# The second norms' variances and inverse deviations, four tiles at a time, on GpSimd instead of VectorE

## The reference

```python
h = patches(x) @ W                                   # 64 images, 36 tokens each, 192 channels
h = h + attention(layernorm(h))                      # 12 heads of 16, causal over the 36 tokens
h = h + experts(layernorm(h))                        # 8 experts, 192 -> 768 -> 192, the best 2 per token
# layernorm: (x - mean) / sqrt(var + 1e-5), over the 192 channels, no weights
```

## Time and profile before

| | |
|---|---|
| time, median of 3 runs | 413.14 us (410.65 to 414.38) |
| profiled execution | 408.58 us, its span 406.8 us |
| TensorE busy | 367.6 us, 90% |
| VectorE busy | 255.3 us, 63% |
| ScalarE busy | 218.6 us, 54% |
| GpSimd busy | 167.7 us, 41% |
| mean granted TensorE clock | 0.964 |

### The profile page before, as it was taken

The page is one execution under the profiler, slowest core; times in us unless marked ns, Lnnn a source line. Parts: engine busy times, 40 slices in busy tenths (PEclk is TensorE's granted clock), DMA queues, the critical chain, the costliest instruction groups (busy, mean ns, idle before and its releaser), DMA issues.

```text
span 406.8 us, 14803 instructions
## 1 busy us (share of the span) xinstructions
PE 367.6 (90%) x5699; PEld 327.6 (81%) x5699; DVE 255.3 (63%) x687; ACT 218.6 (54%) x442; POOL 167.7 (41%) x203
## 2 busy tenths in 40 slices
PE   3989999989999999899897999999999999999910
PEld 3989989979889999885453689999999999999800
DVE  3696477787877867788686254555545554455426
ACT  5667687768777687662344244444444444444400
POOL 8116333345375532422100555555555555553310
PEclk9999999999999899999896999999999999999975
DMA  8974024432334223443060213222223222122058
GB/s 264 314 247 156 15 56 133 135 95 75 118 111 119 84 59 111 117 132 86 27 171 12 60 31 90 61 81 61 80 60 90 81 60 81 60 55 47 31 205 337
DMA packets 29705, 42.81 MB, mean 105 GB/s; under 512 B 12416, under 2 KB 19440, under 8 KB 29640
## 3 DMA queue, kind: packets, MB, share of 16 engines
q1 hardware_dynamic: 25512, 33.37, 27.1%
q0 software_dynamic: 4128, 8.50, 7.4%
HBM read 30.23 MB, written 9.67 MB: 98 GB/s over the span
## 4 chain that ended last, share of the span: by engine, by line
PE 75%; DVE 14%; DMA 3%; ACT 3%; issue 2%; POOL 2%; SPq 0%; POOLq 0%; DVEq 0%; ACTq 0%
PE PSA L1415 19%; PE PSA L1430 15%; PE PSA L1169 6%; PE PSA L1111 6%; PE PSA L1143 5%; PE PSA L1195 4%; PE PSA L1264 4%; PE PSA L1219 3%; PE PSA L1155 2%; PE PSA L1434 2%; PE PSA L1180 2%; PE PSA L1382 2%; DMA W2l<-yrows 2%; DVE H L1098 1%; PE PSA L1164 1%
## 5 line engine op out<-in xcount | busy, mean ns | idle before, releaser
L1415 PE MATMUL PSA<-YT,W1h 128*128 128x128 f16 x774 | 78.0, 219 | 1.5 <-DVE YT L1060 1.5
L1415 PE MATMUL PSA<-YT,W1l 128*128 128x128 f16 (+1 forms) x516 | 75.3, 220 | 0.0
L1430 PE MATMUL PSA<-W2h,PTR 128*128 x516 | 70.9, 246 | 0.3 <-DVE PTR L744 0.3
L543 POOL DMA_INDIRECT yrows<-KBR x43 | 43.1, 1001 | 63.4 <-DVE KBR L1075 63.4
L1415 PEld LDWEIGHTS PSA<-YT,W1h 128*128 x774 | 63.7, 98 | 5.6 <-DVE YT L1060 1.8
L1430 PE MATMUL PSA<-W2l,PTR 128*128 x258 | 63.5, 246 | 0.0
L730 ACT ACTIVATE PTR<-PSA 128x768 f32<-128x768 f32 x43 | 34.9, 812 | 51.1 <-PE PSA L1415 51.1
L538 POOL DMA_INDIRECT REG<-xrows,KBR x43 | 42.4, 987 | 43.6 <-DVE KBR L1050 27.4
L735 ACT ACTIVATE PTR<-PTR 128x768 f16<-128x768 f32 x43 | 36.3, 845 | 44.3 <-PE PSA L1434 44.2
L744 DVE SCALAR_TENSOR_TENSOR PTR<-PTR 128x768 f16<-128x768 f32 x43 | 41.2, 958 | 24.8 <-ACT PTR L735 24.8
L1075 DVE TENSOR_SCALAR KBR<-PSA,KBR 128x192 f32<-128x192 f32 x43 | 17.9, 417 | 52.9 <-PE PSA L1434 52.9
(11 more groups left out here) (179 smaller groups left out, 798.5 us busy)
## 6 DMA issues: line engine op xcount, KB each, us to landing
WSTG<-w SPq DMA_DIRECT2D x16, 384.0 KB, 3.9
WSTG<-w SPq DMA_DIRECT2D x16, 336.0 KB, 3.3
REG<-xt SPq DMA_DIRECT2D x12, 324.0 KB, 4.6
W1l<-xt SPq DMA_DIRECT2D x10, 324.0 KB, 6.8
VB<-VP SPq DMA_DIRECT2D x99, 19.1 KB
H<-hrows SPq DMA_DIRECT2D x6, 288.0 KB, 2.8
xrows<-REG SPq DMA_DIRECT2D x2, 800.2 KB
hrows<-H SPq DMA_DIRECT2D x1, 1296.0 KB
```

Of the source, the lines that this page charges most:

```text
L543: gp.indirect_dma_start(out=yrows, out_offset=bass.IndirectOffsetOnAxis(ap=TARGET[:, s:s + 1], axis=0), in_=YO[s % 2], in_offset=None).the ...
L1415: ins = nc.tensor.matmul(bank(2 * u + f // (FC // 2), 128, FC // 2 * ST_)[:, w:w + ST_], weights[a, c], YT[0:rows, at:at + ST_], start=k = ...
L1430: nc.tensor.matmul(bank(4 + u, ST_, C), GP[a][:, at:at + ST_], weights[b], start=(f, a, b) == (0, 0, 0), stop=False)
```

## The change

For groups 2 to 5, GpSimd computes what VectorE's `variances` and `refine` did. GpSimd's version has twelve operations instead of ten: each of the two fused operations of VectorE (square with a factor, add with multiply) is two. It runs them in the group step behind `norm1_row` and ahead of `norm2_row`. In between it waits for ScalarE's logarithm and exponential, which now wait for GpSimd's seventh operation. Groups 6 and 7 and the first norm stay on VectorE; the counts of VectorE's semaphores are shifted accordingly (`on_vector`).

```diff
+        ON_GPSIMD = range(2, group(PAIRED))
+        PSTEPS = 12
...
+            def group_variances(n):
+                a, b = NORMS[n]
+                base = PSTEPS * (n - ON_GPSIMD.start)
+                gp.wait_ge(st2_done, b - NT)
+                s = ST[:, a * 6:b * 6].rearrange("p (t c) -> p t c", c=6)
+                mean, dm, var = MEAN[:, a:b], DM[:, a:b], VAR[:, a:b]
+                nc.gpsimd.tensor_tensor(mean, s[:, :, 1], s[:, :, 4], ALU.add).then_inc(group_done, 1)
+                nc.gpsimd.tensor_tensor(dm, s[:, :, 1], s[:, :, 4], ALU.subtract).then_inc(group_done, 1)
+                nc.gpsimd.tensor_tensor(var, s[:, :, 2], s[:, :, 5], ALU.add).then_inc(group_done, 1)
+                gp.wait_ge(group_done, base + 2)
+                nc.gpsimd.tensor_tensor(dm, dm, dm, ALU.mult).then_inc(group_done, 1)
+                gp.wait_ge(group_done, base + 4)
+                nc.gpsimd.tensor_scalar(dm, dm, 0.25 * C, None, ALU.mult).then_inc(group_done, 1)
+                nc.gpsimd.tensor_scalar(mean, mean, 0.5, None, ALU.mult).then_inc(group_done, 1)
+                gp.wait_ge(group_done, base + 5)
+                nc.gpsimd.tensor_tensor(var, var, dm, ALU.add).then_inc(group_done, 1)
+                gp.wait_ge(group_done, base + 7)
+                nc.gpsimd.tensor_scalar(HV[:, a:b], var, -0.5 / (C * S_X ** 2), -0.5 * EPS / S_X ** 2, ALU.mult, ALU.add).then_inc(group_done, 1)
+
+            def group_refine(n):
...
+                gp.wait_ge(ln_done, 2 * n + 2)
+                gp.wait_ge(group_done, base + 8)
+                nc.gpsimd.tensor_tensor(t1, rs, HV[:, a:b], ALU.mult).then_inc(group_done, 1)
+                gp.wait_ge(group_done, base + 9)
+                nc.gpsimd.tensor_tensor(t1, t1, rs, ALU.mult).then_inc(group_done, 1)
+                gp.wait_ge(group_done, base + 10)
+                nc.gpsimd.tensor_scalar(t1, t1, 1.5, None, ALU.add).then_inc(group_done, 1)
+                gp.wait_ge(group_done, base + 11)
+                nc.gpsimd.tensor_tensor(rs, t1, rs, ALU.mult).then_inc(group_done, 1)
+
             def norm2_row(t):
-                need(gp, rs_done, group(t) + 1)
+                if group(t) in ON_GPSIMD:
+                    gp.wait_ge(group_done, PSTEPS * (group(t) - ON_GPSIMD.start + 1))
+                else:
+                    need(gp, rs_done, on_vector(group(t)) + 1)
...
                 if has(i + 6):
                     norm1_row(i + 6)
+                if group_end(i - 2) and group(i - 2) in ON_GPSIMD:
+                    group_variances(group(i - 2))
+                    group_refine(group(i - 2))
                 for t in norm2_at(i):
                     norm2_row(t)
...
             def inverse_deviation(n):
                 a, b = NORMS[n]
-                act.wait_ge(mv_done, 9 * n + 7)
+                if n in ON_GPSIMD:
+                    act.wait_ge(group_done, PSTEPS * (n - ON_GPSIMD.start) + 7)
+                else:
+                    act.wait_ge(mv_done, 9 * on_vector(n) + 7)
...
                     stats2(i - 2)
-                    if group_end(i - 2):
+                    if group_end(i - 2) and group(i - 2) not in ON_GPSIMD:
                         variances(group(i - 2))
...
-                if group_end(i - 2):
+                if group_end(i - 2) and group(i - 2) not in ON_GPSIMD:
                     refine(group(i - 2))
```

More of the change, by code:

```diff
@@ L215, in build @@
         st_done, st2_done, mv_done, ln_done, rs_done = [sem(n) for n in ("st_done", "st2_done", "mv_done", "ln_done", "rs_done")]
+        group_done = sem("group_done")
         n1_row, n1_hi, n1_lo, n1_mm, n1_done = [sem(f"norm1_{n}") for n in ("row", "hi", "lo", "mm", "done")]
@@ L345, in build, with on_vector @@
         NORMS += [(NT + t, NT + min(t + GROUP, NT)) for t in range(0, NT, GROUP)]
+        ON_GPSIMD = range(2, group(PAIRED))
+        PSTEPS = 12
+        def on_vector(n):
+            return n - len(ON_GPSIMD) if n >= ON_GPSIMD.stop else n
         def up_biases(p):
@@ new lines, in group_refine @@
+            def group_refine(n):
+                a, b = NORMS[n]
+                base = PSTEPS * (n - ON_GPSIMD.start)
+                rs, t1 = RS[:, a:b], DM[:, a:b]
+                gp.wait_ge(ln_done, 2 * n + 2)
[7 more added lines that the diff above has]
+                nc.gpsimd.tensor_tensor(rs, t1, rs, ALU.mult).then_inc(group_done, 1)
@@ L774, in variances @@
                 nc.vector.tensor_tensor(var, s[:, :, 2], s[:, :, 5], ALU.add).then_inc(mv_done, 1)
-                dve.wait_ge(mv_done, 9 * n + 3)
+                dve.wait_ge(mv_done, 9 * on_vector(n) + 3)
                 nc.vector.tensor_scalar(mean, mean, 0.5, None, ALU.mult).then_inc(mv_done, 1)
                 nc.vector.scalar_tensor_tensor(dm, dm, 0.25 * C, dm, ALU.mult, ALU.mult).then_inc(mv_done, 1)
-                dve.wait_ge(mv_done, 9 * n + 5)
+                dve.wait_ge(mv_done, 9 * on_vector(n) + 5)
                 nc.vector.tensor_tensor(var, var, dm, ALU.add).then_inc(mv_done, 1)
-                dve.wait_ge(mv_done, 9 * n + 6)
+                dve.wait_ge(mv_done, 9 * on_vector(n) + 6)
                 nc.vector.tensor_scalar(HV[:, a:b], var, -0.5 / (C * S_X ** 2), -0.5 * EPS / S_X ** 2, ALU.mult, ALU.add).then_inc(mv_done, 1)
@@ L787, in refine @@
                 nc.vector.tensor_tensor(t1, rs, HV[:, a:b], ALU.mult).then_inc(mv_done, 1)
-                dve.wait_ge(mv_done, 9 * n + 8)
+                dve.wait_ge(mv_done, 9 * on_vector(n) + 8)
                 nc.vector.tensor_tensor(t1, t1, rs, ALU.mult).then_inc(mv_done, 1)
-                dve.wait_ge(mv_done, 9 * n + 9)
+                dve.wait_ge(mv_done, 9 * on_vector(n) + 9)
                 nc.vector.scalar_tensor_tensor(rs, t1, 1.5, rs, ALU.add, ALU.mult).then_inc(rs_done, 1)
@@ L839, in late_rows @@
             def late_rows(t):
-                dve.wait_ge(rs_done, group(t) + 1)
+                dve.wait_ge(rs_done, on_vector(group(t)) + 1)
                 if t == PAIRS[1][0]:
```

## The result

| | before | after |
|---|---|---|
| median | 411.97 us (4 runs) | 421.19 us (4 runs, 419.77 to 423.18) |
| ratio | | 1.0221, 95% interval 1.0144 to 1.0297 |
| profiled execution | 408.58 us, span 406.8 | 419.86 us, span 417.9 |
| mean granted clock | 0.964 | 0.958 |

Medians are of all runs; ratios leave out executions more than 1.5% above the fastest of the same kernel.

The account below looks back on a forecast made before the run. TensorE sets the pace, held up only in four group-ending steps by VectorE and GpSimd. Waits of 0.66 us in two groups and 0.46 in two add 2.2 us to the 413.14 median: 415.4 us, range 408.7 to 420.5.

Parts of the forecast that it names:

- The chain: TensorE alone in most pipeline steps; through VectorE and then GpSimd only in steps that end a group of four tiles.
- Operations of 0.19 us: Estimated length of one GpSimd arithmetic operation on four columns, bounded by 0.11 us from below and 0.306 from above.
- the seven in a row: GpSimd's seven operations that ScalarE waits for take 1.19 us together, not counting the time shut out.
- The shut-out beside VectorE's two-input operations: GpSimd's first operation stands until VectorE's two weight operations end, about 1.8 us; 1.61 us pair in the last two groups.
- the rival without shut-out: GpSimd's four-column operations get through beside VectorE's weight pair; each group gains 1.1 us, 408.7 us in all; chance 0.15.
- The rival of an opening between the two weight operations: GpSimd is let in after VectorE's first weight operation; -0.8 us a group, 412.3 us in all; chance 0.11.
- The logarithm: ScalarE's `inverse_deviation`, waiting for GpSimd's seventh operation, starts 2.03 us later, as does all behind it up to `y_hi`.
- The waits, +2.2 us: TensorE's later projection and transposes add 0.66 us in each of the first two groups, 0.46 in the other two.
- the 1.45 us: TensorE's two waits per group step in the kernel before: 0.72 us at the projection, 0.73 at the second norm's transposes.
- Forecast with the clock as before, or one more fall: Main case: TensorE's clock falls as before or behind one more gap, +2.2 to +3.9 us; chance 0.44.
- the price of a fall: TensorE's clock at its lower level behind one group's gap costs 1.7 us, read from the third group.
- clock or dearer operations: Further clock falls behind group gaps, or longer GpSimd operations, bring the change beyond +4.1 us; chance 0.30.

Follow-up runs that it names:

- a_behind: The changed kernel with VectorE's two weight operations of each group step moved behind `y_lo`: 423.77 us, ratio 1.0278 of before.
- b_warm: The kernel before with three unused matmuls put into TensorE's order ahead of the late projection behind each group: 409.94 us, ratio 0.9960.
- a_warm: The changed kernel with nine unused matmuls put into TensorE's order ahead of the late projection behind each of the four groups: 412.64 us, ratio 1.0004.
- b_gap: The kernel before with five unused statistics operations on VectorE ahead of `y_lo` in each of the four group steps: 423.36 us, ratio 1.0251.
- a_flip: The changed kernel with VectorE's weight pieces dealt the other way round, one in odd steps (all group steps) and two in even: 417.16 us, ratio 1.0135.
- a_late_log: The changed kernel with ScalarE's logarithm and exponential moved behind `y_hi` in its order: 431.64 us, ratio 1.0538.

## Why the prediction was wrong

**What held.** The chain was the one described. Operations of 0.19 us were measured at 0.19 to 0.24, and the seven in a row, 1.19 by the prediction's sum, at 1.35 where nothing shut them out (a_behind). The shut-out beside VectorE's two-input operations ended with the pair, as forecast (the pair at 112.67, the shut-out operation at 112.73), and the rival without shut-out fell: a_behind shows the same twelve operations at 0.2 us each without the pair. The rival of an opening between the two weight operations was half right: exactly one GpSimd operation gets through at the joint in the first two groups, which saves nothing, since the next one stands until the end. The logarithm was expected to wait until 2.03 us later than before within its step; it came 113.60 - 107.55 = 6.05 behind `shift` instead of 109.05 - 105.17 = 3.88, that is 2.17 later. In this group `stats2` came 2.75 behind `shift` instead of 2.40, which is 0.35 of it (why is open); the two operations that got through gave some 0.2 back.

**The waits, +2.2 us, measured +2.8.** The account with the clock held gives 0.54, 0.82, 0.76 and 0.64 where the prediction had 0.66, 0.66, 0.46 and 0.46. The last two are larger because the kernel before waits less there than the 1.45 us that I took from the second group for all four: b_warm's groups 4 and 5 are 0.19 and 0.38 us shorter than its group 3.

**The step that failed: "Forecast with the clock as before, or one more fall".** The prediction saw what the gap would become (1.95 us; it was 2.13) and the price of a fall (1.7 us; 64.71 - 57.44 = 7.3 us for four, 1.8 each). But it counted one fall in four gaps of 0.72 us as the rate for gaps three times as long, and put four falls at the edge of the range under "clock or dearer operations", 0.30. The measured sum is 2.76 for the waits, plus 7.27 for four falls, less 0.74 for the fall that before had already: 9.29 us. That the price was nearly right is in part luck: group by group (after less a_warm) a fall cost 1.45, 1.38, 2.92 and 1.52 us, and the one in before, from which the 1.7 was read as clock lost, lengthened its groups by 0.74 only. a_warm and b_gap show that this is the clock and not GpSimd: the first takes it away and leaves the waits, the second makes it with VectorE alone. In a_flip even gaps of 1.04 to 1.54 us have it fall four times in four. Nor were the four gaps before alike, as the prediction took them: that of the earlier trace rows is 0.65 us without work, and the other three are

```profile
85.76 0.29 PE L1219 MATMUL PSA<-WOh,YT 97*108 97x192 f16 x1 [0.97 <-DVE YT L744]
...
137.93 0.29 PE L1219 MATMUL PSA<-WOh,YT 97*108 97x192 f16 x1 [0.45 <-DVE YT L744]
...
164.69 0.29 PE L1219 MATMUL PSA<-WOh,YT 97*108 97x192 f16 x1 [0.45 <-DVE YT L744]
```

The clock fell behind the third, one of the two shortest. So "one in four" of one execution was no rate for longer gaps, and the three that left the clock alone were weak evidence against.

## What to carry to other kernels

Where TensorE sets the pace, price a new wait twice: as a wait, and as a gap in which the clock can fall; here the second was worth more than twice the first, and unused matmuls in the gap gave nearly all of it back. Before work moves to GpSimd, look at which VectorE operations with two SBUF inputs will run beside it, for in these runs GpSimd mostly stood until they ended, however small its own work was. And a shorter list on the busier engine is no gain if its successor, in another engine's fixed order, must wait for the slower one.

## What the runs showed of the hardware that was not expected

- Without the unused matmuls, the clock fell at all twelve waits for the projection in after, b_gap and a_flip (1.04 to 2.27 us), but also at 0.45 (before) and 0.62 (a_behind) and not at 0.97 (before). At the second norm's transposes it fell at four waits of seven between 1.42 and 1.93 us (a_behind, a_late_log). What decides beside the length stays open, and the counts are of one profiled execution of each kernel.
- At its lower level the clock stayed for very different lengths: 3 to 7 us behind the gaps of after, but up to 14 in b_gap and a_late_log and 17 in a_behind. What decides it stays open.
- GpSimd's first operation of a group slipped through although VectorE's began 0.10 us behind it (110.74 and 110.84), while nearly the same offset in the third group (VectorE's pair of W2 0.10 behind 138.77) cost 1.78 us. In the trace before, GpSimd's larger operations were shut out by VectorE starting up to 0.29 us behind.
- VectorE was never seen to wait for GpSimd: its weight pair took 1.83 us with three GpSimd operations at it, and 1.81 without.
